# ScalarE makes the third value part of two pairs in each batch of four, in place of one: a graph layer and mixture-of-experts kernel on one core

## What is computed

```
xn  = layernorm(x)
e   = exp(edge_weight - max)                     # one value for each edge
row_sum = segment_sum(e, src)
a   = e / (row_sum[src] + 1e-6)
out0 = segment_sum(a * M[dst], src);  out1 = segment_sum(a * M[src], dst)   # M = xn @ Wm + bm
gnn = relu(relu(layernorm([out0, out1] @ W1 + b1)) @ W2 + b2)
x   = x + gnn + linear_attention(xn)
x   = x + expert_ffn(layernorm(x))               # 8 experts, each row goes to one
```

## Time and profile before

| | us |
|---|---|
| median of three runs | 508.72 |
| the profiled execution, its own time | 508.95 |
| its span (first to last instruction) | 507.2 |
| PE busy | 446.9 (88%) |
| DVE busy | 394.9 (78%) |
| ACT busy | 296.3 (58%) |
| POOL busy | 192.0 (38%) |
| the stage that builds `adj`, about 232 to 323 us | 91.0 |

### The profile page before, as it was taken

One profiled execution on the slowest core, in us unless ns is written; L12 is line 12 of the kernel. 1 busy time (PEld: TensorE's weight loads), 2 busy tenths in 40 slices (PEclk: granted clock), 3 DMA queues, 4 the chain that ended last, 5 costly groups with the idle time before them and its releaser, 6 DMA issues.

```text
span 507.2 us, 9248 instructions
## 1 busy us (share of the span) xinstructions
PE 446.9 (88%) x2871; PEld 371.5 (73%) x2871; DVE 394.9 (78%) x830; ACT 296.3 (58%) x836; POOL 192.0 (38%) x157
## 2 busy tenths in 40 slices
PE   4189999999998999998889899799999946999992
PEld 1067888888877887986777777698987745788881
DVE  6859989999978886979999999678459774456652
ACT  0497566666662324975887778855335562466540
POOL 0188887788886887810000000000000008255321
PEclk9789999999999999999999999899999857999995
DMA  7980000000000000022000000000006964233210
GB/s 193 294 297 3 1 3 3 3 2 2 2 2 3 3 1 3 2 68 118 1 3 1 2 3 1 2 1 1 0 1 230 421 217 118 77 115 108 68 62 15
DMA packets 15778, 31.09 MB, mean 61 GB/s; under 512 B 7686, under 2 KB 8317, under 8 KB 14709
## 3 DMA queue, kind: packets, MB, share of 16 engines
q1 hardware_dynamic: 9237, 23.21, 13.6%
q0 software_dynamic: 6496, 7.31, 7.4%
HBM read 24.90 MB, written 7.38 MB: 64 GB/s over the span
## 4 chain that ended last, share of the span: by engine, by line
PE 48%; DVE 24%; ACT 10%; issue 8%; DMA 5%; SPq 3%; POOL 1%; DVEq 0%; POOLq 0%; ACTq 0%
PE banks L539 25%; DVE s_hot L1225 9%; PE banks L849 6%; ACT row_1h L1519 4%; PE banks L721 3%; DVE s_one L1209 3%; DMA rec<-in_x 3%; SPq L381 3%; PE banks L714 2%; PE banks L610 2%; PE banks L840 2%; DMA x_rows<-factors 1%; PE banks L573 1%; PE banks L702 1%; DVE stat L1296 1%
## 5 line engine op out<-in xcount | busy, mean ns | idle before, releaser
L461 POOL DMA_INDIRECT slots<-record,row_i x118 | 154.8, 1312 | 64.7 <-issue 64.7
L472 POOL DMA_INDIRECT rec<-x_rows,get_i x17 | 20.0, 1174 | 202.8 <-DMA x_rows<-factors 197.9
L702 PE MATMUL banks<-d_hot,s_hot 128*128 128x251 bf16 x648 | 80.2, 275 | 4.7 <-DVE s_hot L1225 4.4
L1575 ACT ACTIVATE adj<-banks x108 | 60.4, 585 | 22.2 <-PE banks L702 18.6
L702 PEld LDWEIGHTS banks<-d_hot,s_hot 128*128 128x128 bf16 x648 | 55.0, 97 | 15.1 <-issue 6.0
L539 PE MATMUL banks<-w_hi,xT_hi 128*125 128x512 f32 (+1 forms) x160 | 59.5, 372 | 0.8 <-DVE bia L1059 0.4
L539 PE MATMUL banks<-w_lo,xT_hi 128*125 128x512 f32 (+1 forms) x160 | 58.5, 366 | 0.0
L539 PE MATMUL banks<-w_hi,xT_lo 128*125 128x512 f32 (+1 forms) x160 | 58.5, 366 | 0.0
L1490 ACT ACTIVATE q_sb<-q_sb,hmax 125x64 f32<-125x64 f32 x80 | 26.7, 335 | 36.3 <-DVE hmax L1078 36.3
L1225 DVE TENSOR_TENSOR s_hot<-s_one,parts 128x1024 bf16<-128x1024 bf16 (+2 forms) x84 | 47.9, 623 | 0.0
L539 PEld LDWEIGHTS banks<-w_hi,xT_hi 128*125 128x125 f32 x160 | 29.7, 185 | 7.1 <-issue 1.6
(11 more groups left out here) (300 smaller groups left out, 1071.7 us busy)
## 6 DMA issues: line engine op xcount, KB each, us to landing
w_raw<-in_w2f SPq DMA_DIRECT2D x4, 1024.0 KB, 9.4
w_raw<-in_wqkv SPq DMA_DIRECT2D x3, 1024.0 KB, 18.9
rec<-in_x SPq DMA_DIRECT2D x2, 1120.0 KB
x_rows<-rec SPq DMA_DIRECT2D x10, 224.0 KB
w1a<-in_w1f SPq DMA_DIRECT2D x1, 2048.0 KB, 8.6
w1b<-in_w1f SPq DMA_DIRECT2D x1, 2048.0 KB, 16.5
b_sb<-in_b2f SPq DMA_DIRECT2D x1, 2048.0 KB, 22.9
slots<-record,row_i POOLq DMA_INDIRECT x118, 2.6
```

The lines of the kernel that those rows point to most:

```text
L461: pool.indirect_dma_start(slots, bass.IndirectOffsetOnAxis(ap=row_i[:, c:c + 1], axis=0), record[:, c, :], None).then_inc(slot_st, 16)
L472: pool.indirect_dma_start(rec_c[:, c % RING, :], None, x1_rows, bass.IndirectOffsetOnAxis(ap=get_i[:, c:c + 1], axis=0)).then_inc(ld_rec[c ...
L702: mm = pe.matmul(flat_banks[:, bass.ds(at_in, AW)], s_hot[:, n % DB, i, q, :, j], d_hot[:, n % DB, q, :, j], start=False, stop=(i == WT - ...
L1575: act.activation(adj[:, bass.ds(w, BW2)], flat_banks[0:TP, bass.ds(out_at, BW2)], ACT.Copy).then_inc(win_ok, 1)
```

## The change

ACT makes the third value part of the last two pairs (c and d) of each batch, in place of the last alone. `AQ` = 2 is the number of such pairs. DVE's third multiplication shrinks from three pairs to two (L1224), `low_hot` issues four ACTIVATEs in place of two, and PE waits for ACT's part at the third pair of a batch in place of the fourth. The position of `low_hot` in ACT's order stays.

```diff
-PB, DB = 4, 4
+PB, DB, AQ = 4, 4, 2
...
-                if q == PB - 1 and n >= 1:
+                if q == PB - AQ and n >= 1:
                     pe.wait_ge(act_hot, n)
...
-                    m = k - 1 if i == WT - 1 and k == PB and n >= 1 else k
+                    m = k - AQ if i == WT - 1 and k == PB and n >= 1 else k
...
                 for j in range(2):
-                    last = act.activation(s_hot[:, n % DB, WT - 1, PB - 1, :, j], s_one[:, n % 2, PB - 1, :, j], ACT.Copy,
-                                          scale=low_f[:, c + j:c + j + 1])
+                    for q in range(PB - AQ, PB):
+                        a = c + j - 2 * (PB - 1 - q)
+                        last = act.activation(s_hot[:, n % DB, WT - 1, q, :, j], s_one[:, n % 2, q, :, j], ACT.Copy,
+                                              scale=low_f[:, a:a + 1])
                 last.then_inc(act_hot, 1)
```

## The result

| | before | after |
|---|---|---|
| median, us | 508.28 | 510.62 |
| ratio, 95% interval | | 1.0048 (1.0027 to 1.0069) |
| profiled execution: span, us | 507.2 | 508.7 |
| matmuls of the stage (L702), from the first to the last start, us | 232.0 to 322.5: 90.5 | 232.0 to 324.9: 92.9 |

The change makes the kernel slower, by 0.48% or 2.4 us (1.4 to 3.5); 2.5 us was forecast. In the profiled execution the stage that builds `adj` is 2.4 us longer. The span is only 1.5 us longer, since what follows the stage took 0.9 us less in this one execution than in the one of before. The eleven profiles of this document take 179.6 to 184.7 us from the last matmul of the stage to the end of the span. So in what follows the length of the stage carries the argument and the medians confirm it.

A forecast was written before the change was run, and what follows sets the result against it. DVE was taken to set the pace at 3.386 us a batch. After the change a 3.495 us loop through ACT and PE, over 24 turns, ends the stage 2.5 us later: from 508.72 to 511.2 us, range 508.0 to 513.0.

The forecast's parts named there:

- DVE's saving: DVE's third multiplication in batches 1 to 25 goes from 768 to 512 elements, 549 to 413 ns: 0.136 us a batch.
- The loop: Copy c, PE's pair b of the next batch, its copy, four ACTIVATEs, copy c again: 3.495 us a batch; chance 0.69.
- the two proxies: For PE waiting on a copy: ACT-to-PE signal 0.14 us, seen behind the stage; reset to first matmul, queue empty, 0.13.
- From the loop to the stage: b1 at 236.19 us plus 24 turns puts b25 at 320.07, before 317.59; the stage ends 2.5 us later.
- PE's waits: At pair b's reset PE waits some 0.6 us for ACT's copy in batches without a load of 16, else almost nothing.
- PE's earlier wait for `act_hot`: PE waits for ACT's part one pair earlier in each batch; claimed to cost nothing.
- DVE idles late: DVE waits for `low_hot` ahead of `s_one` only from batch 16 or so, idling about 2 us.
- Is anything else later than the loop?: Check of other waits on ACT, PE and DVE: ACT's copy d, load, copies a and b take 1.63 against 1.845 us.
- ACT's own sequence: Four copies, four ACTIVATEs and one load on ACT: 3.28 us a batch; if it came last, 506.0 us.
- slower by more: Rival: more ACTIVATEs in a row or a second load delay copy c, 3.55 us a batch, 512.5 us; chance 0.04.
- PE's own need: PE alone would need about 3.1 us a batch: 2.84 for its pairs, and 0.41 for each load of 16.
- faster: Rival: only DVE's pace counts, 3.25 us a batch, the stage ends 3.4 us earlier, 505.3 us; chance 0.13.

The follow-up runs named there:

- e3: Kernel before with only DVE's third multiplication cut to two pairs, pair c's third value part left out; ratio 0.9937, stage 87.4 us.
- e2: Kernel before with two more ACTIVATEs in `low_hot`, written to a spare tile nobody reads; ratio 1.0037, stage 93.0 us.
- e6: Kernel before with four more ACTIVATEs in `low_hot`, six in a block, the added ones to a spare tile; ratio 1.0334, stage 107.4 us.
- e1: Changed kernel with the four ACTIVATEs split, two ahead of copy c and two ahead of copy d; ratio 1.0011 to before, stage 91.2 us.
- e7: Changed kernel with the ACTIVATEs split in two pairs and PE's load of 16 made two of 8; ratio 0.9913 to before, stage 87.4 us.
- e5: Kernel before with one more ACTIVATE in `low_hot`, three in a block, written to a spare tile; ratio 0.9991, stage 90.6 us.
- e8: Kernel before with PE's load of 16 values made two loads of 8, nothing else; ratio 1.0007, stage 90.6 us.

## Why the prediction was right, step by step

- **DVE's saving.** 0.136 us a batch was forecast. The third multiplication is recorded 128x512 in all 25 batches, and e3 turned it into 3.1 us of the stage. Right; the row of the kernel after (busy us, mean ns), beside the earlier trace rows:

```profile
L1225 DVE TENSOR_TENSOR s_hot<-s_one,parts 128x512 bf16<-128x512 bf16 x31 | 12.7, 420 | 0.0
```

- **The loop.** Forecast 3.495 us for a turn, measured 3.495 as a mean of 24. That the two agree to the last digit is luck: the common turn is 3.48, and the one long turn of 3.77, which nobody forecast, makes up the difference. The step that no row showed, PE waiting for a copy within the stage, cost what the two proxies gave: from the start of copy c to PE's reset 0.71 against 0.585 + 0.14, and 0.13 to the first matmul. e2 and e6 show that it is this loop, by its slope (0.29 us for an ACTIVATE and batch) and by its threshold, between three and four ACTIVATEs.
- **From the loop to the stage.** b25 was forecast at 320.07 and is at 320.08; the last pair at about 324.4 and is at 324.34. Without the long turn they would have come 0.3 us earlier, which still is the forecast.
- **PE's waits.** Where the batch's first pair has no load of 16, pair b comes 0.4 to 0.6 us late in most cases (a distance of 1.31 us between the matmuls at 262.81 and 264.12, in place of 0.71); the waits show about 0.3 of it, since a matmul's record reaches into the pause. In the other batches up to 0.18 is left (266.71 to 267.60 is 0.89). Right, if the second is called "almost nothing".
- **PE's earlier wait for `act_hot`** costs nothing: e2 has the loss without it.
- **DVE idles late.** Forecast from batch 16 on, some 2 us. `s_one` keeps its 3.25 us up to batch 14 (274.38), comes 0.1 us late in batch 15, and from batch 16 on goes in steps of 3.48 (281.22, 284.70, 288.18). The waits give only one wait for it, 1.5 us at the end, because the small gaps of 0.2 us are hidden between overlapping records. The starts give the amount: batch 25 starts at 312.53, and 11 steps of 3.25 from 274.38 would put it at 310.13, so DVE has idled 2.4 us by then. Both the turning point and the amount were right.
- **"Is anything else later than the loop?"** This part was incomplete, though the forecast didn't need what was missing. I compared loops of one batch only. The loop over two batches through PE's load takes 6.78 us, and for the kernel after it is the next in line, 3.39 against 3.495. Had the block been two ACTIVATEs twice, I would have forecast a gain of 2.5 us or more, and been wrong, as the expectation of e1 was.
- **ACT's own sequence** was put at 3.28 us for a batch, with 0.55 + 0.14 for the register load between copy d and copy a. This step was wrong: the load costs nothing there. In the timeline of e1 above, copies d, a and b stand in one row (269.77, three in 1.53 us), 0.47 apart although a load of 549 ns lies between d and a, and where ACT doesn't wait, copies c are 3.05 us apart. It changes nothing in the forecast, since the loop was longer either way, but "slower by more", which needed this load in the loop, has nothing for it in these runs.
- **PE's own need** was put at about 3.1 us a batch, with 0.41 us for each load of 16. The 0.41 is the gap in the record. The starts give 1.33 to 1.41 us from pair to pair across that load in most batches of e3, in place of 0.71, and 0.81 to 0.89 across the load of 8, which was left out. By these starts PE needs 3.2 to 3.3 us a batch (an estimate), about as much as DVE's new 3.25. So the 3.4 us of the rival "faster" had no slack left on PE, as e3 shows with its 3.1.
- **The rule of the Trainium skill** (the page "Perfetto Trace Analysis", section "Optimizing Scalar/DVE Operations", on offloading from a saturated DVE) says that the move may make sense. The move costs time in this kernel as the change stands (2.4 us), and gives time in e7, where the same work was moved to the same engine in two pieces and PE's load was made shorter. On what the "may" depends, here on who waits behind the receiving engine, the section leaves open.

## What to carry to other kernels

An engine with free time can still be on a loop: add up the way from the end of its instruction to whoever waits for it and back, for as many steps as the buffers in between allow, and compare the sum with the pace of the bottleneck before you give the engine more to do. Work that is moved is best put in pieces between the instructions that others wait for, not in a block; here the same four ACTIVATEs made the stage 2.4 us longer as a block and, with one more obstacle removed, 3.1 us shorter in two pieces. When the pace then stays above the sum, look for a loop of more than one period, above all where something happens only every second time.

## What the runs showed of the hardware

- A register load holds PE's queue, and its length goes with the number of values: 1105 ns for 16, 591 for 8. Seen from the matmuls, a pair ahead of which 16 are loaded comes 1.41 us after the one before it (e1, 271.32 to 272.73), with 8 loaded 0.89 us (e1, 268.08 to 268.97), without a load 0.71. Some 0.4 us of each is thus hidden behind the matmuls in flight, and halving the load takes away most of what is seen. How much is seen isn't the same everywhere: in e6, where PE waits for a copy in every batch, it is mostly 1.15 to 1.28 us and 0.70 to 0.81.
- On ACT a load of 8 values (548 ns) costs nothing while ACTIVATEs ahead of it are in flight: in e6 copy a starts 0.47 us behind copy d in each of the batches 1 to 25, as two copies do without a load between them.
- Behind the stage PE pauses for 2.97 us in each of these kernels, and its granted clock differs afterwards in a way that doesn't go with the change. Some 10 us from the restart of PE's transposes, in windows of before, after and e5 (length, busy us of PE, PEld, DVE, ACT and POOL, granted clock, DMA share, GB/s):

```profile
325.80:335.80 10.00, 10.00 (x54) 9.23 (x55) 6.39 (x12) 6.19 (x12) 0.00 (x0) 0.83 0.01 2
```

```profile
328.00:338.00 10.00, 9.85 (x43) 8.89 (x44) 5.10 (x10) 5.24 (x9) 0.00 (x0) 0.68 0.01 2
```

```profile
325.90:335.90 10.00, 9.98 (x63) 9.34 (x64) 7.91 (x14) 7.44 (x12) 0.00 (x0) 1.00 0.01 2
```

A mean of 0.83 is one part of the stretch at the lower of the two levels (1.2 GHz) and the rest at 2.4 GHz; 1.00 is all at 2.4. This was the other unknown of the prediction, put at 1 us to either side. After has the longer low part of the two and yet takes 0.9 us less behind the stage than before, so this isn't what makes it slower; within the stage the clock is granted in full in both (1.00). The low part is missing in e1, e2, e3 and e5, which take 179.6 to 182.9 us from the last matmul of the stage to the end; the other seven take 182.3 to 184.7. So it is likely one reason why the spans of single executions scatter around what the stage says, but not the only one: with it e8 takes 182.3 us, without it e3 takes 182.9.
